# One half of eight gather tiles of each round fetched row by row by SyncE in a two-round graph network on one NeuronCore

## The reference

```python
def _round(x, w, b, gamma, beta, src, dst, etype):
    h = jax.nn.relu(_bn(x, gamma, beta))              # normalised over the nodes
    h = jnp.einsum('nd,od->no', h, w) + b             # (N, T*D)
    h3 = h.reshape(N, T, D)
    msg = h3[src, etype]                              # one row of 128 floats for each edge
    return jax.ops.segment_sum(msg, dst, num_segments=N)
h_new = _round(features, w1, b1, g1, be1, src, dst, etype)
h_new = _round(h_new, w2, b2, g2, be2, src, dst, etype)
...
x = _layernorm(x + _L0_gnn_ref(...))                  # adds h_new + features
h = x @ W_in
W_ij = (ssp(f_ij[:, 0, :] @ Wf1 + bf1) @ Wf2 + bf2) * f_ij_cutoff
out = jax.ops.segment_sum(h[idx_j] * W_ij, idx_i, num_segments=x.shape[0])
x = _layernorm(x + ssp(out @ Wo1 + bo1) @ Wo2 + bo2)
```

## Time and profile before

| | |
|---|---|
| runs | 6475.83 us median of 3 (6472.38 to 6478.03) |
| the profiled execution | 6482.43 us, span 6480.6 us |
| PE busy | 4158.0 us (64%) |
| POOL busy | 4619.0 us (71%) |
| DVE busy | 3822.2 us (59%) |
| ACT busy | 1611.9 us (25%) |
| DMA | 726.45 MB, mean 112 GB/s |

### The profile page before, as it was taken

One profiled execution on the slowest core, in us unless ns is written; L12 is line 12 of the kernel. 1 busy time (PEld: TensorE's weight loads), 2 busy tenths in 40 slices (PEclk: granted clock), 3 DMA queues, 4 the chain that ended last, 5 costly groups with the idle time before them and its releaser, 6 DMA issues. The chain is left out here.

```text
span 6480.6 us, 66649 instructions
## 1 busy us (share of the span) xinstructions
PE 4158.0 (64%) x17271; PEld 2806.2 (43%) x17271; DVE 3822.2 (59%) x7438; ACT 1611.9 (25%) x3872; POOL 4619.0 (71%) x4787
## 2 busy tenths in 40 slices
PE   7445454544445645455454555778777889999898
PEld 4333343433334434334343444333323346666696
DVE  6544444443334777776676666544444457777698
ACT  4000000000001200000000000576666656666504
POOL 5777777777777677777777777577777777777604
PEclk9555555555556755655555676898898889999999
DMA  9211121212223521221222333333333356777696
GB/s 342 53 52 52 52 53 52 52 52 55 65 65 117 188 52 52 53 52 52 52 52 53 86 90 92 99 117 110 110 110 110 110 174 217 220 219 216 208 315 211
DMA packets 432604, 726.45 MB, mean 112 GB/s; under 512 B 104654, under 2 KB 206576, under 8 KB 431506
## 3 DMA queue, kind: packets, MB, share of 16 engines
q1 hardware_dynamic: 281652, 400.74, 19.7%
q0 software_dynamic: 150592, 321.58, 17.0%
HBM read 509.16 MB, written 212.75 MB: 111 GB/s over the span
## 5 line engine op out<-in xcount | busy, mean ns | idle before, releaser
L573 POOL DMA_INDIRECT edge_rows<-messages,idx_stage x1504 | 1446.1, 961 | 487.1 <-issue 457.9
L1658 PE MATMUL banks<-onehot,edge_rows 128*128 128x128 f32 x3008 | 715.9, 413 | 995.7 <-DMA edge_rows<-messages,idx_stage 960.8
L1658 PEld LDWEIGHTS banks<-onehot,edge_rows 128*128 128x128 f32 x3008 | 613.8, 303 | 1117.2 <-DMA edge_rows<-messages,idx_stage 1082.0
L630 POOL DMA_INDIRECT sorted_rows<-edge_rows,idx_stage x784 | 760.3, 970 | 276.3 <-issue 238.2
L630 POOL DMA_INDIRECT sorted_rows<-buf_a,idx_stage x784 | 760.5, 970 | 260.5 <-issue 241.4
L573 POOL DMA_INDIRECT buf_x<-messages,idx_stage x747 | 717.4, 960 | 227.7 <-issue 227.7
L573 POOL DMA_INDIRECT buf_a<-messages,idx_stage x747 | 714.5, 957 | 227.7 <-issue 227.7
L1040 DVE TENSOR_TENSOR buf_a<-buf_a,banks 128x128 f32 x375 | 108.1, 288 | 1044.3 <-PE banks L1658 1005.4
L689 ACT ACTIVATE h_stage<-banks,bn_shift,bn_scale 128x128 f32<-128x128 f32 x128 | 58.6, 458 | 2521.1 <-PE banks L1599 2521.1
L1658 PE MATMUL banks<-x_onehot,buf_x 128*128 128x128 f32 x1494 | 355.9, 413 | 490.6 <-DMA buf_x<-messages,idx_stage 490.5
L1658 PE MATMUL banks<-x_onehot,buf_a 128*128 128x128 f32 x1494 | 344.8, 403 | 459.9 <-DMA buf_a<-messages,idx_stage 459.5
(11 more groups left out here) (201 smaller groups left out, 7088.3 us busy)
## 6 DMA issues: line engine op xcount, KB each, us to landing
buf_a<-sorted_rows SPq DMA_DIRECT2D x593, 288.0 KB, 4.0
messages<-work SPq DMA_DIRECT2D x196, 320.0 KB
buf_a<-dst_rows SPq DMA_DIRECT2D x198, 256.0 KB
buf_a<-in_attr SPq DMA_DIRECT2D x198, 128.0 KB, 2.5
buf_a<-h_in SPq DMA_DIRECT2D x396, 64.0 KB
edge_rows<-messages,idx_stage POOLq DMA_INDIRECT x1504, 2.5
sorted_rows<-edge_rows,idx_stage POOLq DMA_INDIRECT x784
sorted_rows<-buf_a,idx_stage POOLq DMA_INDIRECT x784
```

What stands on the lines that cost most here:

```text
L573: nc.gpsimd.indirect_dma_start(gathered[p][h][:, t, :], None, source, bass.IndirectOffsetOnAxis(ap=idx_stage[:, h, t:t + 1], axis=0),).the ...
L630: nc.gpsimd.indirect_dma_start(sorted_rows, bass.IndirectOffsetOnAxis(ap=idx_stage[:, 2 * u + h, t:t + 1], axis=0), msg_halves[2 * u + h][ ...
L1658: last = nc.tensor.matmul(ps_sums[p][slot][j], rows_in_slot[:, j * GROUP_TILES + t, :], hot[:, j * GROUP_TILES + t, :], start=(t == 0), st ...
```

## The change

Half 140 of each round (`FETCHED = (2 * 70,)`, iteration 70, slot 0) is no longer gathered by GpSimd. SyncE fetches its 1024 rows: for each of the 128 partitions it loads, twice, four row numbers from `msg_idx` into registers and issues four DMAs of one row (512 bytes) each, into a buffer of its own (`fetched`: in `buf_x` in round 0, in `buf_a` in round 1). `fetch_half(rnd)` is written on SyncE right behind the round's message stores. TensorE reads that buffer for half 140 and waits for its semaphore. In round 1 the buffer lies over the filter inputs, so `load_attributes` now stands behind `load_x(1)` and its wait, and the row of ones is written ahead of iteration 74. Some pairs of semaphores are folded into one. The rest of the diff keeps the branch `beyond` in step.

```diff
+FETCHED = (2 * 70,)
...
+        FETCH_ROWS = COLS_HALF * 16
+        FETCH_TURN = FETCHED[0] // GATHER_SLOTS
...
+        def fetch_tile(engine, kind, p, i, e, t):
+            rows = table[p].rearrange("n (t d) -> (n t) d", t=T)
+            at = nc.values_load_multi_w_load_instructions(
+                msg_idx[e:e + 1, FETCHED[i] * HALF_TILES + t:FETCHED[i] * HALF_TILES + t + 4], engines=[kind], min_val=0,
+                max_val=N * T - 1, skip_runtime_bounds_check_because="a source times the types plus a type")[1]
+            for j in range(4):
+                engine.dma_start(fetched[p][i][e:e + 1, t + j, :], rows[ds(at[j], 1), :]).then_inc(s_fetched[p][i], 16)
...
+            def fetch_half(p):
+                sp.wait_ge(s_setup, RANGE_LINKS + 2)
+                for q in range(SLOTS):
+                    sp.wait_ge(s_row_out[q], rows_out(p, q))
+                for e in range(P):
+                    for t in range(0, HALF_TILES, 4):
+                        fetch_tile(nc.sync, mybir.EngineType.SP, p, 0, e, t)
+
             for rnd in range(2):
...
+                fetch_half(rnd)
                 if rnd == 0:
 
                     sp.wait_ge(s_bias_split, 5)
...
             sp.wait_ge(s_short_out, 32)
-
-            for q in range(SLOTS):
-                sp.wait_ge(s_row_out[q], rows_out(1, q))
...
             load_x(0)
+            sp.wait_ge(s_y, 1)
+            load_x(1)
             for h in range(2):
                 load_attributes(h, h)
-            sp.wait_ge(s_y, 1)
-            load_x(1)
             store_chunk(0)
...
                         pool.wait_ge(s_idx[p], r * GATHER_SLOTS + (h + 1))
+                        if r * GATHER_SLOTS + h + 2 * RAW_ITERS[p] in FETCHED:
+                            continue
...
+            def filter_ones():
+                nc.vector.memset(f_sb[RBF:RBF + 1, :, :, :], 1.0).then_inc(s_cut, 1)
...
             def rank_round():
                 hots_ahead(1)
                 round_loop(1, buf_x, RAW_ITERS[1], CHUNK_ITERS, None, False)
+                filter_ones()
...
-                if p == 1:
-                    nc.vector.memset(f_sb[RBF:RBF + 1, :, :, :], 1.0).then_inc(s_cut, 1)
...
-                    pe.wait_ge(s_gather[2 * u + h][j], gathers(p, 2 * u + h, j, turn + 1))
+                    if source is None:
+                        pe.wait_ge(s_gather[slot][j], gathers(p, slot, j, turn + 1, after or isinstance(r2, int) and r2 > FETCH_TURN))
+                    else:
+                        pe.wait_ge(s_fetched[p][source], FETCH_ROWS)
```

More of the change, by code:

```diff
@@ L95 @@
 assert all(n % 2 == 0 and (2 * HALF_TILES // 2 + 1) * n + HALF_TILES + 2 <= CHUNK_ITERS + RAW_TILES for n in RAW_ITERS)
+assert all(2 * max(RAW_ITERS) <= k < 2 * CHUNK_ITERS for k in FETCHED)
 assert X_COLS * X_PARTS == N and X_COLS % BN_CHUNK == 0 and GROUPS % 4 == 0
@@ L194, in gnn_program @@
         raw_rows = [c[:, 0:RAW_TILES * P].rearrange("p (t n) -> p t n", n=P) for c in (buf_x, buf_a)]
+        fetched = [[c.rearrange("p (t n) -> p t n", t=HALF_TILES) for c in (
+            spare[:, at + half_cols * (2 + i):at + half_cols * (3 + i)] for i in range(len(FETCHED)))]
+            for spare, at in ((buf_x, RAW_ITERS[0] * ITER_TILES * P), (buf_a, RAW_ITERS[1] * ITER_TILES * P))]
         row_stages = [buf_a[:, i * WIDE:(i + 1) * WIDE] for i in range(6, CHUNKS)] + [
@@ L282, in gnn_program @@
         s_parts_in, s_bias_split = sem("bias_rows_in"), sem("bias_split")
-        s_bn, s_bn_sd = [sem(f"bn_step_{i}") for i in range(2)], [sem(f"bn_sd_{i}") for i in range(2)]
+        s_bn, s_bn_sd = [sem(f"bn_step_{i}") for i in range(2)], sem("bn_sd")
         s_h_ready = [sem(f"h_ready_{i}") for i in range(2)]
@@ L287, in gnn_program @@
         s_row_out = [sem(f"rows_out_{q}") for q in range(SLOTS)]
-        s_clear = [sem(f"acc_cleared_{i}") for i in range(2)]
+        s_clear = sem("acc_cleared")
         s_idx = [sem(f"idx_ready_{i}") for i in range(3)]
         s_gather = [[sem(f"gathered_{h}_{j}") for j in range(2)] for h in range(GATHER_SLOTS)]
+        s_fetched = [[sem(f"fetched_{p}_{i}") for i in range(len(FETCHED))] for p in range(2)]
         s_onehot = [sem(f"onehot_ready_{i}") for i in range(2)]
@@ L306, in gnn_program @@
         s_ps_iota, s_first = sem("iota_in_psum"), sem("first_places_step")
-        s_hot = [sem(f"high_onehot_{i}") for i in range(2)]
+        s_hot = sem("high_onehot")
         s_count, s_paired, s_picked, s_passed, s_placed, s_placed_out = (sem(n) for n in (
@@ L321, in gnn_program @@
         s_prod, s_turned = sem("products_ready"), sem("products_turned")
-        s_tagged, s_part = sem("rows_tagged"), sem("partitions_in_psum")
+        s_tagged = sem("rows_tagged")
         s_scat = [sem(f"scattered_{i}") for i in range(MSG_SLOTS)]
@@ L347, in rows_out, with gathers @@
             return ((each if stores is None else stores) + (1 + rnd * each)) * 16
-        def gathers(p, h, j, n):
+        def gathers(p, h, j, n, after=False):
             missing = 0 if h < GATHER_SLOTS - 1 else GROUP_TILES - LAST_TILES if j == 0 else GROUP_TILES
@@ L352, in gathers @@
             done = n * GROUP_TILES - (missing if isinstance(n, int) and n == turns_of[p] else 0)
-            return (done + p * (turns_of[0] * GROUP_TILES - missing)) * 16
+            skipped = GROUP_TILES * len([k for k in FETCHED if k % GATHER_SLOTS == h])
+            return (done + p * (turns_of[0] * GROUP_TILES - missing - skipped) - (skipped if after else 0)) * 16
+        FETCH_ROWS = COLS_HALF * 16
+        FETCH_TURN = FETCHED[0] // GATHER_SLOTS
+        assert all(k // GATHER_SLOTS == FETCH_TURN for k in FETCHED)
+        def fetch_tile(engine, kind, p, i, e, t):
[5 more added lines that the diff above has]
+                engine.dma_start(fetched[p][i][e:e + 1, t + j, :], rows[ds(at[j], 1), :]).then_inc(s_fetched[p][i], 16)
         def turns(engine, first, end, rolled=False):
@@ L610, in _ @@
             gather_raw(0)
-            nc.gpsimd.memset(buf_a[:, :], 0.0).then_inc(s_clear[0], 1)
+            nc.gpsimd.memset(buf_a[:, :], 0.0).then_inc(s_clear, 1)
             for rnd in range(2):
@@ L617, in _ @@
                     pool.wait_ge(s_closed, 2)
-                    nc.gpsimd.memset(buf_x[:, :], 0.0).then_inc(s_clear[1], 1)
+                    nc.gpsimd.memset(buf_x[:, :], 0.0).then_inc(s_clear, 1)
                 gather_pass(rnd, table[rnd].rearrange("n (t d) -> (n t) d", t=T),
@@ L668, in _ @@
                 act.wait_ge(s_bn[rnd], N // BN_CHUNK + 1)
-                nc.scalar.activation(bn_tmp[:, 0:1], bn_mv[:, 1:2], ACT.Sqrt, bias=eps_col[:, 0:1]).then_inc(s_bn_sd[rnd], 1)
+                nc.scalar.activation(bn_tmp[:, 0:1], bn_mv[:, 1:2], ACT.Sqrt, bias=eps_col[:, 0:1]).then_inc(s_bn_sd, 1)
                 act.wait_ge(s_bn[rnd], N // BN_CHUNK + 5)
@@ L888, in batch_norm @@
                 link(nc.vector.bn_aggr(bn_mv[:, :], bn_cols[rnd]))
-                dve.wait_ge(s_bn_sd[rnd], 1)
+                dve.wait_ge(s_bn_sd, rnd + 1)
                 dve.wait_ge(s_const_in, CONSTANTS * 16)
@@ L932, in build_high @@
                     src_high[:, ds(it * ITER_TILES + h * HALF_TILES, HALF_TILES)].unsqueeze(2).broadcast_to(shape),
-                    ALU.is_equal).then_inc(s_hot[p], 1)
+                    ALU.is_equal).then_inc(s_hot, 1)
             def count_lanes(k, h, j, i):
-                dve.wait_ge(s_hot[0], k + 1)
+                dve.wait_ge(s_hot, k + 1)
                 dve.wait_ge(s_count, k * 2 + (j + 1))
@@ L946, in pair_lanes @@
             def pair_lanes(k, h, i):
-                dve.wait_ge(s_hot[1], k + 1)
+                dve.wait_ge(s_hot, k + (2 * ITERS + 2))
                 dve.wait_ge(s_passed, k + (i + 1))
@@ L1294, in round_pass @@
             def round_pass(p):
-                dve.wait_ge(s_clear[p], 1)
-                if p == 1:
-                    nc.vector.memset(f_sb[RBF:RBF + 1, :, :, :], 1.0).then_inc(s_cut, 1)
+                dve.wait_ge(s_clear, p + 1)
                 dve.wait_ge(s_row_ready[p], BLOCKS + SLOT3)
@@ L1437, in _ @@
             y_chunk(CHUNKS_IN)
-            nc.vector.tensor_copy(ps_part, part_f[:, :]).then_inc(s_part, 1)
+            nc.vector.tensor_copy(ps_part, part_f[:, :]).then_inc(s_ps_iota, 1)
             stage_cutoff(0, 0)
             dve.wait_ge(s_cut, 2)
-            dve.wait_ge(s_part, 1)
+            dve.wait_ge(s_ps_iota, 3)
             spread_half(0, 0)
@@ L1634, in raw_beyond, with aggregate @@
                     sum_beyond(p, raw_rows[p][:, half * HALF_TILES:(half + 1) * HALF_TILES, :], half)
-            def aggregate(p, r2, u, h, beyond, between=None):
+            def aggregate(p, r2, u, h, beyond, between=None, after=False):
                 r = r2 * 2 + u
@@ L1640, in aggregate @@
                 slot = 2 * u + h
-                rows_in_slot = gathered[p][slot]
+                source = FETCHED.index(r * 2 + h) if isinstance(r2, int) and r * 2 + h in FETCHED else None
```

(12 more changed lines are left out.)

## The result

The changed kernel takes 7010.8 us (median of 5, 6998.2 to 7012.3) against 6475.3 for the kernel before (now five runs, with the three of the table above): ratio 1.0825, 95% interval 1.0813 to 1.0837. It is 535 us slower; 7042 was forecast, in a range of 6975 to 7310.

The account below looks back on a forecast made before the run. GpSimd's gathers were taken as the bound. A hold of +587 us less 20.2 saved gave +566: 7049 us on the profiled execution, 7042 for the median after its 6.6 us offset; range 6975 to 7310.

Parts of the forecast that it names:

- The step that decided it: Round 0, TensorE's flag load: waits for bias rows now issued after the fetch, so no aggregation until then; GpSimd held 587 us.
- Four halves are the whole cover: Round 0: GpSimd fills its four slots (32 gathers), then VectorE, ScalarE and GpSimd all end up behind TensorE.
- Nothing recovers: Round 0 after the hold: GpSimd is again the bound at 10.08 us per half, so the 587 us stay lost.
- T - 29.4: GpSimd's hold in round 0, resuming at T + 177.0 instead of 206.4: forecast 587 us.
- T: Time of one round's fetch on SyncE: 256 groups of 2.405 us, forecast 616 us; bounds 561 and 879.
- L375's 0.280: Issue time in us of a one-row load on SyncE, used for the lower bound of a round's fetch, 561 us.
- The distance between DMAs, 0.185: SyncE's fetch: us from the end of one row DMA to the next, derived from eight L474 DMAs.
- The saving of 20.2 us: GpSimd, both rounds: 16 gathers removed at 1.26 us each, taken whole because GpSimd is the bound.
- The 4 us allowed for slower gathers: Round 1: row DMAs share DMA engines with the gathers; at most 4 us, counted for the range only.
- The rival of dearer rows: Same hold, rows at L406's price or with straight-line code stalls, fetch up to 879 us: 7305 us; chance 0.13.
- those of a slower engine: Fetch rows limited by the DMA engine, about 7810 us, chance 0.05; or each awaiting its landing, about 10350, chance 0.02.
- If the fetch took over 1333 us this cover would be gone: Round 1: fetch of 616 us has 1333 until half 140; loads of x behind it have 800 us of cover left.

## Why the prediction was right

The step that decided it, that the three bias rows would stand behind 1024 DMAs and TensorE behind the bias rows, is shown: from the traces, and by undoing it in two ways, the bias rows first (on an undisturbed chip too) and the wait moved (on slower chips only). "Four halves are the whole cover" and "Nothing recovers" hold too: the hold was T - 29.4 to within 0.1 us in three runs.

The term that was mis-sized is T: 616 us forecast, 586 measured. On the profiled executions the miss is 37 us (7049 forecast, 7011.6 measured), and T is 30 of them. That the median's miss is only 31 is luck: the forecast took off 6.6 us, by which the profiled execution of before lay above its median, and that of after lies 0.8 above. Within T, too, two errors partly cancelled. Lines L372 and L368 of the profile after, against the earlier trace rows:

```profile
L372 SPq DMA_DIRECT2D buf_x<-messages x1024: 224/225/336, 161.8 to 747.3; - x171
...
L368 SPq TENSOR_LOAD <-msg_idx x512: 457/562/740, 161.2 to 3301.5; - x171
```

A one-row DMA took 0.225 us in place of 0.333, and that is even below L375's 0.280, which I had used as the bound; the mean is 0.234, since the first of a group takes 0.26. 1024 x 0.099 = 101 us less. The register load took 0.562 in place of 0.303, 256 x 0.26 = 66 us more: its price goes with its place, and in the convolution, where L468 was read, no one-row DMAs stand ahead of it. The distance between DMAs, 0.185, was right. The sum, -35, leaves +5 for small gaps. Here the row that I took (L468) misled and the Trainium skill was nearer: its "DMA: Bandwidth & Descriptors", "Latency and other measured facts", has about 600 ns for `tensor_load`, and of these loads the trace agrees, with 0.562. The fixed cost of about 2 us that the prediction also takes from the Trainium skill stands there for DMAs that GpSimd issues; SyncE's rows left every 0.57 us.

The saving of 20.2 us is confirmed, within the intervals, by the kernels in which nothing hides it: 21.3 for 16 gathers, 40.2 for 32. Round 1 was hidden, as forecast; the row of ones and the filter inputs moved to 4127.7 and 4130.7 with no trace on the path. The 4 us allowed for slower gathers didn't appear: their median is 0.952 in the changed kernel against 0.955 before.

In the profiled execution the 529.2 us are: +557.1 hold, -20.2 gathers, -2.6 from an earlier first gather (161.8 against 164.4), and -5.1 that remain. The gathers that are left were on average 2 to 4 ns shorter than before, 8 us in all, and the stages outside the rounds 3 us longer. The unchanged kernel's gathers weren't profiled again, so it isn't shown that the change has a part in this.

The rival of dearer rows and those of a slower engine were wrong for the chips of the first executions. But the prediction's "If the fetch took over 1333 us this cover would be gone" came true on the slower chips, by another mechanism than any I had priced: SyncE itself stalled while the other engines worked. It isn't shown what stalls it.

## What to carry to other kernels

An engine with nothing to do for 1400 us is not free to use if a short transfer stands behind the long one in its list: look for the next item of that list, then for who waits on it, before pricing the work. Price idle time by the first consumer behind it, not by the consumer of the new work. And work on an idle engine that fits with only a factor of two to spare can be hidden on one chip and not on another.

## What the runs showed of the hardware that was not expected

- SyncE issues a DMA of one row of 512 bytes in 0.213 to 0.225 us and one over 128 partitions in 0.333; with the address arithmetic between them one row goes out every 0.41 us, and with the loads every 0.57.
- A register load of four numbers took 0.30 us in the convolution and 0.56 in the fetch, behind one-row DMAs; each further number of the load 0.058. Right behind another load it took 0.31 us from partitions 0 to 63 and 0.47 from 64 to 127.
- Of four chips in these series three ran the unchanged kernel in 7846 to 7859 us in place of 6474, and the same 1024 row DMAs beside the running round took 1540 to 1627 us in place of 574 to 589. With eight numbers a load they took 1579 there, and 564 with the other engines held.
